# Turning v with DMA transposes instead of TensorE, beside a second inverse stream and a planner that orders by the work still ahead

## The reference

```
h = layernorm(x) * (1 + ca) + sa
q, k, v = silu(causal_dwconv4(h @ W{q,k,v}))          # 4 heads of 256, conv of 4 taps per channel
beta = sigmoid(h @ Wb)
# delta rule, per head: A = tril(k_beta k^T, -1) in chunks, T = inv(I + A)
u = T v_beta - (T k_beta) S ;  o = q S + tril(q k^T) u ;  S = S + k^T u
local_mix = p0 * v + p1 * fir3(v) + p2 * fir31(v)      # short and long filter per channel
o = g * o + (1 - g) * local_mix ;  o = rmsnorm(o) @ Wo
x = x + ga * o
h = layernorm(x) * (1 + cb) + sb
x = x + gb * tanh(h @ W1 @ W2 @ W3 + bias)
```

## Time and profile before

| | us |
|---|---|
| median of 3 runs | 823.68 (821.15 to 824.53) |
| the profiled execution | 824.18 |
| its span, first to last instruction, of its slowest core | 822.5 |
| PE busy | 721.5 (88%) |
| DVE busy | 614.6 (75%) |
| ACT busy | 415.5 (51%) |
| POOL busy | 191.8 (23%) |

### The profile page before, as it was taken

How to read it: one execution, slowest core, us unless ns; L and a number is a source line. 1 busy time by engine, 2 the same in 40 slices (tenths; PEclk the granted TensorE clock), 3 DMA queues, 4 the chain that set the end, 5 groups by cost and what they waited for, 6 DMA issues and landing times.

```text
span 822.5 us, 17847 instructions; the slowest of 8 cores (809.5 to 822.5 us)
## 1 busy us (share of the span) xinstructions
PE 721.5 (88%) x5888; PEld 478.8 (58%) x5888; DVE 614.6 (75%) x1555; ACT 415.5 (51%) x899; POOL 191.8 (23%) x167
## 2 busy tenths in 40 slices
PE   3779978799988887888989989889999889989996
PEld 1234466677776665676767767667767655434432
DVE  3534774688787887886888887789887789976875
ACT  1122425766574744665665647667555555422222
POOL 0000001134205612551341133034133223210100
PEclk9899988999999999999999999999999999999999
DMA  8989959754615252343635421421326859298853
GB/s 239 321 238 327 275 184 249 189 73 91 80 33 111 45 90 83 61 72 53 104 52 69 55 60 53 67 82 45 69 38 144 153 119 192 53 229 188 220 169 141
DMA packets 121486, 105.14 MB, mean 128 GB/s; under 512 B 68926, under 2 KB 102261, under 8 KB 121014
## 3 DMA queue, kind: packets, MB, share of 16 engines
q1 hardware_dynamic: 98150, 89.29, 43.1%
q0 software_dynamic: 20944, 10.53, 11.3%
q10 hardware_dynamic: 2304, 4.20, 1.5%
HBM read 79.38 MB, written 18.89 MB: 119 GB/s over the span
## 4 chain that ended last, share of the span: by engine, by line
PE 55%; DMA 15%; DVE 12%; issue 8%; ACT 5%; SPq 2%; POOL 2%; DVEq 0%; ACTq 0%; POOLq 0%
PE ps L907 13%; PE ps L953 7%; PE ps L1534 6%; PE ps L1588 5%; DMA z_k<-wmod 4%; DMA kst<-w 4%; PE ps L1306 2%; PE ps L676 2%; DMA w1t_sb<-wv 2%; DVE S L1425 2%; PE ps L1270 2%; DMA h<-xn 2%; PE ps L1396 1%; PE ps L1417 1%; PE ps L1129 1%
## 5 line engine op out<-in xcount | busy, mean ns | idle before, releaser
L907 PE MATMUL ps<-h,wq_sb 128*128 128x256 bf16 x512 | 69.7, 284 | 2.3 <-ACT wq_sb L524 2.1
L907 PE MATMUL ps<-h,wk_sb 128*128 128x256 bf16 x512 | 69.2, 279 | 0.4 <-ACT kst L966 0.4
L907 PE MATMUL ps<-h,wv_sb 128*128 128x256 bf16 x512 | 69.2, 275 | 0.1
L1588 PE MATMUL ps<-wq_sb,h 128*128 128x512 bf16 x256 | 60.7, 380 | 0.0
L1534 PE MATMUL ps<-wk_sb,ofm 128*128 128x512 bf16 x256 | 58.6, 379 | 2.1 <-DMA ofm<-o_d 2.1
L1248 POOL TENSOR_TENSOR eb<-vtm 128x1024 bf16<-128x1024 bf16 x16 | 34.1, 2128 | 111.7 <-ACT vtm L370 93.2
L1254 POOL TENSOR_SCALAR vbs<-vtm,gt 128x256 bf16<-128x256 bf16 x64 | 60.0, 949 | 0.0
L907 PEld LDWEIGHTS ps<-h,wq_sb 128*128 128x128 bf16 x512 | 50.9, 102 | 13.2 <-issue 3.9
L907 PEld LDWEIGHTS ps<-h,wk_sb 128*128 128x128 bf16 x512 | 49.4, 100 | 9.1 <-issue 1.1
L907 PEld LDWEIGHTS ps<-h,wv_sb 128*128 128x128 bf16 x512 | 49.1, 98 | 8.7 <-issue 0.5
L1093 DVE TENSOR_TENSOR E<-Qc,cb_sb 128x512 bf16<-128x512 bf16 x96 | 44.5, 463 | 10.6 <-DVE Qc L1144 0.9
(11 more groups left out here) (243 smaller groups left out, 1858.7 us busy)
## 6 DMA issues: line engine op xcount, KB each, us to landing
xs<-x SPq DMA_DIRECT2D x16, 512.0 KB, 6.8
mst<-wmod POOLq DMA_DIRECT2D x16, 512.0 KB, 7.4
xf<-x SPq DMA_DIRECT2D x16, 512.0 KB, 5.6
out<-xf SPq DMA_DIRECT2D x16, 512.0 KB, 2.7
w1t_sb<-wk SPq DMA_DIRECT2D x8, 512.0 KB, 10.2
w1t_sb<-wq SPq DMA_DIRECT2D x8, 512.0 KB, 7.1
w1t_sb<-wv SPq DMA_DIRECT2D x8, 512.0 KB, 6.7
o_d<-ob ACTq DMA_DIRECT2D x16, 256.0 KB, 2.8
```

Source lines behind the costliest of these rows:

```text
L907: (lambda e, g=g: e.matmul(bk[:, 256 * i:256 * (i + 1)], wt[:, 2048 * p + 256 * g + 128 * i:2048 * p + 256 * g + 128 * (i + 1)], hv[:, 256 ...
L1588: (lambda e, g=g: e.matmul(bk[:, :], h2[n % 3][:, 128 * g:128 * (g + 1)], wq_sb[:, 1024 * g + 512 * half:1024 * g + 512 * half + 512], sta ...
```

## The change

Five things are changed together.

1. **v is turned by DMA.** `vtokens` is split into `vturns`, which issues 8 DMA transposes of 128x128 per chunk from SP into vtm, and `vshort`, which keeps only the short filter on PE (6 matmuls of 128 columns per head). The identity columns and the 64 copies out of PSUM are gone; `sdiag` has 24 diagonal matrices and no copies of the identity.
2. **Two inverse streams**, `inverse(0)` and `inverse(1)`, for even and odd chunks, each with its own Ab, Lb, E, NN; Qc and cmp now lie in NN.
3. **The planner** lays the program out twice without emitting, takes from each layout the length of the modelled work that follows each step (`tails_of`), and the third layout picks, among the steps of the engine whose earliest step starts first, the one with the longest way left (`pick`). SLACK is 0, and `first` no longer counts in the last layout.
4. **Buffers**: vbs is single (a chunk's is written after the previous chunk's L1422), and the normalised rows are written over xs in place, always by ACT; so the loads of the next x wait until these rows have been transposed.
5. **PSUM**: output and feed-forward products share a cap of 3 banks (`ring_o`) in place of 8.

```diff
-    SLACK = 150.0
+    SLACK = 0.0
+    def tails_of(self):
+        tail = [0.0] * len(self.links)
+        out = {}
+        for i in range(len(self.links) - 1, -1, -1):
+            which, work, after = self.links[i]
+            tail[i] += work
+            out[which] = tail[i]
+            for j in after:
+                tail[j] = max(tail[j], tail[i] + self.HOP)
+        return out
...
-                ready.append((start - step.first, len(ready), s, name, start))
...
+            best = self.pick(ready)
+    def pick(self, ready):
+        if self.tails is None:
+            return min(ready, key=lambda r: (r[0] - r[2][1].first, r[1]))
+        first = min(ready)
+        near = [r for r in ready if r[3] == first[3] and r[0] <= max(first[0], self.q[first[3]].at) + self.SLACK]
+        return max(near, key=lambda r: (self.tails.get((r[2][2], r[2][3]), 0.0), -r[1]))
...
+            tails = None
+            for turn in range(2):
+                tails = layout(None, None, tails).tails_of()
+            prog = layout(target, handle, tails)
...
-                    fr = [(yield Need(("x_used", n - 2)))]
+                    fr = yield Need(("xn_used", n // 2 - 1))
...
-                for n in range(NC):
+                Ab, Lb, E, NN = inv_bufs[odd]
+                Qc, cmp = NN[:, 0:128], NN[:, 128:384]
+                for n in range(odd, NC, 2):
...
+            def vturns():
...
+                    t = yield dma("sync", s_vt[n % 2], [fm] + vfree, [(lambda e, m=m: e.dma_start(
+                        vt[:, 128 * m:128 * (m + 1)], vv[:, m, 4 + 128 * c:132 + 128 * c], transpose=True))
+                        for m in range(8)], 2.5e5)
+                    post("vts", n, [t])
+
+            def vshort():
...
                     for h in range(4):
                         mm = yield st("tensor", [sd, fm, hd], lambda bk, h=h: [
-                            fn for i in range(2) for fn in (
-                                lambda e, i=i, m=2 * h + i: e.matmul(
-                                    bk[:, 256 * i:256 * (i + 1)], vv[:, m, 4 + 128 * c:132 + 128 * c],
-                                    sdiag[:, 512 * m:512 * m + 256], start=True, stop=False, skip_group_check=True),
...
+                            (lambda e, i=i, j=j, m=2 * h + i: e.matmul(
+                                bk[:, 128 * i:128 * (i + 1)], vv[:, m, 4 - j + 128 * c:132 - j + 128 * c],
+                                sdiag[:, 384 * m + 128 * j:384 * m + 128 * (j + 1)], start=(i == 0 and j == 0),
+                                stop=(j == 2), skip_group_check=True)) for i in range(2) for j in range(3)],
+                            6 * mmw(128), ring=ring_v)
-                        cv = yield evac([mm] + vfree, o3, bv[:, :, 0, :], 256)
...
-                    sv = [(yield Need(("x_tok", n - 2)))] if n >= 2 else []
+                    sv = [(yield Need(("x_tok", n - 1)))] if n >= 1 else []
```

More of the change, by code:

```diff
@@ L249, in put @@
             inc = 16
+        here = len(self.links)
+        self.links.append((which, work + (self.PIPE if name == "tensor" else 2000.0 + step.land if step.sem else 0.0),
+                           [self.made[tok.sem, tok.value] for tok in step.after]))
+        self.made[done.sem, done.value] = here
         if name == self.target:
@@ L263, in run @@
         live = []
-        for s in streams:
-            live.append([s, next(s)])
+        for i, s in enumerate(streams):
+            live.append([s, next(s), i, 0])
         while live:
-            best = None
             moved = False
@@ L289, in run @@
                 start = self.start_of(step, name)
-                ready.append((start - step.first, len(ready), s, name, start))
[L291 to L298, removed]
+                ready.append((start, len(ready), s, name))
+            if not ready:
                 if moved:
@@ L407, in build_nc @@
         vtm = [sb("vtm%d" % i, 1024) for i in range(3)]
-        vbs = [sb("vbs%d" % i, 1024) for i in range(2)]
+        vbs = sb("vbs", 1024)
         m01 = [sb("m01_%d" % i, 256, F32) for i in range(4)]
@@ L477, in build_nc @@
         s_kt = sem("s_kt")
+        s_vt = [sem("s_vt%d" % i) for i in range(2)]
         s_h = [sem("s_h%d" % i) for i in range(4)]
@@ L1608, in final @@
                             th[n % 2][:, 512 * half:512 * (half + 1)], b, AF.Tanh)], 680)
-                        ring.give(mm.banks[0], t2)
+                        ring_o.give(mm.banks[0], t2)
                         ths.append(t2)
@@ L1624, in residual @@
                     post("out", n, t)
-            prog.run([loads(), setup(), filters(), mod_front(), w123(), xloads(), ln(), recur(), outs_of_recurrence(), norm_of_outputs(), inverse(),
-                      gates(), bfront(), vtokens(), mixing(), vscaled(),
+            prog.run([loads(), setup(), filters(), mod_front(), w123(), xloads(), ln(), recur(), outs_of_recurrence(), norm_of_outputs(), inverse(0), inverse(1),
+                      gates(), bfront(), vturns(), vshort(), mixing(), vscaled(),
                       spectra(), products(), longs(), conv(), proj(), prepare(), next_weights(), last_memory(), cloads(),
                       output(), ln2a(), ln2b(), ffn(), final(), residual()])
-            outs = [prog.board[("out", n)] for n in range(NC - NXF, NC)]
-            if target == "sync":
-                for t in outs:
-                    handle.wait_ge(t.sem, t.value)
+            return prog
         @block.tensor
```

118 lines of the change are left out of this document (55 added, 63 removed).

## The result

The changed kernel takes **880.8 us** (median of 4 runs, 877.4 to 885.3) beside 822.9 us before in the same comparison: 1.071 times the time before, 95% interval 1.065 to 1.077. The chip sometimes runs a kernel in a slower state; all ratios use the fast runs alone, while the times are medians of all runs and stand up to 2.5 us above those of the fast ones. Forecast were 790 us and a range of 770 to 822. The second rival, "the issue of small transposes is dear", came true, and the time lies 42 us beyond even that rival's 839.

A forecast was written before the change was run, and what follows sets the result against it. The middle stage was taken as bound by PE's work plus holes from short dependent chains. 824.2 - 7 (columns) - 25 (order) - 6 (start) + 4.5 (v by DMA) = 790.7, by the median 790 us; range 770 to 822.

The forecast's parts named there:

- The second rival: SP's issues of v's transposes (L1220), felt at L1296: at 1.22 us each the sum is 839 us; chance 0.12.
- v by DMA, +4.5: v's path to its first reader, 5.1 us at 0.3 us an issue; four blocks short, +4.5 us in all.
- The upper bound: v's small transposes on SP: each issue costs 1.22 us like a 128x1024 one, path 12.4 us, 52.6 us in all.
- Seven blocks short by 52.6 us in all: Blocks 0 to 6 at 1.22 us an issue: v's path of 12.4 us outlasts PE's covering work, 52.6 us together.
- is idle most of the stage: SP in the middle stage: its queue has room for 16 issues a block, 5 us at 0.3 each.
- a sign that the prediction had named: Last stage, where chunks 14 and 15 now sit: if it grows, the prediction is wrong.
- Rival 3: Real latencies differ from the planner's, holes move to L1296, L1332 or loads of x: 820 to 828 us; chance 0.10.
- Columns: PE's half-head matmuls lose the identity's columns: 0.055 us for each of 128 halves, -7 us; half-heads 0.165 us apart.
- The order: PE's waits at the inverse and recurrence, 50.6 us, half recovered: -25 us; waits before the round 10 us or less.
- The start: Start of the kernel: weights wq and wv issued sooner, wait for block 0's h mostly covered; -6 us, bounds 0 and -10.
- Edits at nothing: Single vbs, the output stage's cap of 3 banks and the last block's late chunks: counted as no time.
- rival 1: Middle stage held by DVE and ACT, so recovered waits come back at other lines: 815 us; chance 0.18.

The follow-up runs named there:

- Experiment 8: Sixteen DMA transposes a block that nothing reads, added to the kernel with v turned on TensorE (839.8 us; priced in the planner 839.7) or that with one inverse (888.4).
- (6): The changed kernel, its planner counting a chunk's eight transpose issues as 9.2 us of SyncE in place of 60 ns, instructions the same: 822.4 us, 1.001.
- tails_only: The kernel before with the new rule of order alone, one inverse at a time and v turned on TensorE: 792.3 us, 0.966.
- one_inv: The changed kernel with v turned on TensorE and one inverse at a time, the new rule and small edits kept: 770.4 us, 0.934.

## Why the prediction was wrong

**The step that failed** is the term "v by DMA, +4.5". It took 0.3 us for an issue, "near the 0.237 us of a 1 KB DMA, since an eighth of the descriptors is left". The issue took 1.20 us. The upper bound, "each costs what the large one does: 1.22", was the right one. The nearest row was the wrong neighbour: the earlier trace rows is a plain copy, a transpose like the new ones. Likeness of the operation counted and size did not; in the changed kernel a plain load of 512 KB (L841) held SyncE 0.43 us, less than a transpose of 32 KB. The Trainium skill, in "DMA: Bandwidth & Descriptors", section "Rules for kernel authors", says that a transfer under 64 KB pays mostly overhead. For these transposes the trace agrees: 32 KB took SyncE 1.20 us and 256 KB 1.29.

**The mechanism at that price was right, and half the cost.** Seven blocks short by 52.6 us in all, the prediction's own figure at 1.22 us, stand beside 60.6 - 7.8 = 53 us measured before L1296 (the changed kernel against TensorE's turn, whose row in the middle stage is this):

```profile
PEld ps L1296 <- issue: 7.8, 14, 1.3
```

But the turn cost 105 us. The prediction said of SyncE that it "is idle most of the stage", that behind the issues stand "loads of x, needed a block later", and priced them at nothing. Experiment 8 shows that to be the second error: with no reader of v at all the held queue costs 64 to 118 us. In the changed kernel the waits outside v's reader are smaller. Of the 96.6 us between its span and that of TensorE's turn 53 lie before L1296, 15 at the place that follows, 11 are busy time, 6 lie in the start, and some 12 are spread. How much of these is the held queue no run separates. The place of the 15, SyncE:

```profile
716.99 19.79 SPq L1220 DMA_TRANSPOSE vtm<-vfm  x16
736.88 0.45 SPq L726 DMA_DIRECT2D row_d<-rowb  x1
737.50 1.24 SPq L1546 DMA_TRANSPOSE ofm<-o_d  x1
```

and PE, in the same stretch:

```profile
742.12 5.84 PE L1560 MATMUL ps<-wk_sb,ofm 128*128 128x512 bf16 x16 [15.16 <-DMA ofm<-o_d]
```

The last block's sixteen issues stand before the transpose of an output chunk, and PE waits 15.2 us; block 7 had been counted as covered, which held for v and not for SyncE. The last stage grew by 17.4 us, a sign that the prediction had named.

**The planner's price was the third.** Rival 3 said it: "a turn counts as one DMA for it", and holes would move to L1296. They did, and the true price took back 58 of the 105 us (6). The rival was given 0.10 and 820 to 828 us, and the prediction nowhere joined it to rival 2: a dear issue and a planner that counts it as nothing together.

**The clock gave more away.** From 700 to 750 us PE is busy 30 of 50 us at a granted clock of 0.80, part of the time at the lower of its levels (1.2 and 2.4 GHz): 0.67 from 740 to 750 us, after a stretch from 730 in which PE did nothing. The sixteen matmuls after the wait took 5.84 us, 0.37 each, where the 48 before it took 12.21, 0.25 each. No term of the forecast's sum stood for that.

**What held.** *Columns:* twelve matmuls of half-heads take 0.83 us, so 0.055 each and 0.165 a half-head. *The order:* waits before the round 8.4 us; the rule alone gave 30.5 us where 25 was taken. But its cause was told wrongly: the text gave it to the two inverses and the rule together, and one inverse under the new rule does the same (waits before the round of 7.1 and 9.9 us in `tails_only` and `one_inv`). So the gaps don't need the other chunk's rounds to be filled. *The start:* wv went out at 126.4 us, 8.1 us sooner than in the earlier trace rows, as foreseen, in this row of SyncE; what that gave by itself no run shows:

```profile
126.42 15.76 SPq L552 DMA_DIRECT2D w1t_sb<-wv  x8
```

*Edits at nothing:* the three banks 2.2 us with overlapping intervals, so nothing that can be told; the layernorm's rows, counted "as room, not as time", were worth up to 21 us together with the start's 6. *The other rivals:* waits didn't return at the inverse (rival 1). Once v's turn was out of it, the new order did what it planned (rival 3), and all that was left gained 47 us, 18 more than the prediction's sum without the turn.

**The weight of the bounds.** The range of one term was 0.6 to 52.6 us, wider than the gain it stood against, and its upper end rested on the only row of a transpose. A chance of 0.12 for it was too small.

## What to carry over

An operation's issue price is read from rows of the same operation, not of the same size: cut one of these transposes in eight and SyncE is held seven to eight times as long (8 x 1.20 = 9.6 us beside 1.29). A DMA queue's time counts like an engine's: add up each block's issues (here 20 us), then ask for every load and transpose behind them which in-order engine stands still until it lands. A planner's order is only as good as its prices; one entry of 60 ns for 9.2 us cost 58 us. And when a change bundles a gain with a loss, run it with the doubtful part undone: without the turn by DMA and with one inverse this one is 6.6% faster than the kernel before.

## What the runs showed of the hardware

The issue of a DMA transpose on SyncE took 1.20 us for 128x128, 1.22 for 128x256 and 1.29 for 128x1024 (medians), and 1.23 for 128x128 from a source in one piece; from issue to landing it was 2.3 us at 128x128 and 3.5 at 128x1024. The kernel paid 0.83 to 1.02 us for each of them where the planner counted them as nothing, and 0.42 where it had the price. A plain DMA took 0.24 us at 1 KB and 0.43 at 512 KB. The granted clock went down where PE stood still for v: 0.91 over the middle stage, 0.98 in the same kernel with v turned on TensorE.
